# Two reorderings at the head of a mixture-of-experts stage: the first gate/up products on TensorE, the weight preparations on VectorE

## The reference

```
x = x + tanh(g_xattn[0]) * mamba(ctx, layernorm(x), ...)
# mixture of experts: E=64 experts, K=8 of them per token, at most CAP=64 tokens per expert
w, sel = top_k(softmax(layernorm(x) @ gate_w.T), 8); w = w / sum(w)
h   = silu(inp @ wg) * (inp @ wu)          # per expert: (64,256) @ (256,96), twice
out = h @ wd                               # (64,96) @ (96,256)
x = x + tanh(g_ffn[0]) * (sum over the chosen experts of w * out)
x = x + tanh(g_xattn[1]) * attention(layernorm(x), ctx, Wq, Wk, Wv, Wo)
# feed-forward with weight_quant: scale = 1 / mean(|w|); clip(round(w * scale), -1, 1) / scale
x = x + tanh(g_ffn[1]) * bitlinear(layernorm(gelu(silu(bitlinear(layernorm(x), w1)))), w2)
```

## Time and profile before

| | us |
|---|---|
| runs of the kernel | 674.95, 677.10, 678.04 (median 677.1) |
| the profiled execution | 675.54, of which the span is 673.8 |
| expert stage in the profile, from the first indices (218.9) to the last `combine` (329.6) | 110.7 |
| busy over the whole span: TensorE / VectorE / ScalarE / GpSimd | 503.6 / 507.5 / 355.7 / 275.9 |

### The profile page before, as it was taken

One profiled execution on the slowest core, in us unless ns is written; L12 is line 12 of the kernel. 1 busy time (PEld: TensorE's weight loads), 2 busy tenths in 40 slices (PEclk: granted clock), 3 DMA queues, 4 the chain that ended last, 5 costly groups with the idle time before them and its releaser, 6 DMA issues.

```text
span 673.8 us, 10758 instructions
## 1 busy us (share of the span) xinstructions
PE 503.6 (75%) x3144; PEld 371.6 (55%) x3144; DVE 507.5 (75%) x1328; ACT 355.7 (53%) x784; POOL 275.9 (41%) x261
## 2 busy tenths in 40 slices
PE   5935777778695488979779999999999997243232
PEld 3311222223285356757569999999999996022021
DVE  4277999999869856945447977977887886878854
ACT  2474555445176221221446766676676666485483
POOL 4016777788010743530068358538632331110100
PEclk9955999989898597999879999999999999665566
DMA  6907300000023399992412013103200000000000
GB/s 171 216 10 285 97 0 0 0 32 1 8 54 112 97 286 266 285 285 72 145 52 73 9 24 72 33 1 69 56 0 1 1 2 0 0 17 0 16 16 16
DMA packets 43794, 48.53 MB, mean 72 GB/s; under 512 B 5628, under 2 KB 40038, under 8 KB 43494
## 3 DMA queue, kind: packets, MB, share of 16 engines
q1 hardware_dynamic: 39910, 36.46, 19.0%
q0 software_dynamic: 3840, 11.54, 7.2%
HBM read 41.43 MB, written 6.56 MB: 71 GB/s over the span
## 4 chain that ended last, share of the span: by engine, by line
issue 33%; PE 20%; DVE 19%; POOL 14%; DMA 6%; ACT 5%; DVEq 1%; SPq 1%; POOLq 0%; ACTq 0%
DVE hst L1426 6%; POOL G L551 5%; POOL pn L567 5%; DMA wdn<-in_L_ffn_wd 4%; PE ps L1165 3%; PE ps L915 2%; PE ps L1130 2%; DVE hc L1435 2%; PE ps L1150 1%; POOL G L531 1%; PE ps L1206 1%; DVE ebuf L1559 1%; DVE ebuf L1558 1%; PE ps L1208 1%; PE ps L1207 1%
## 5 line engine op out<-in xcount | busy, mean ns | idle before, releaser
L567 POOL TENSOR_TENSOR pn<-pr,pinv 128x512 f32<-128x512 f32 x64 | 66.9, 1046 | 88.5 <-DVE pinv L1794 87.9
L966 PE MATMUL ps<-hc,ident 128*128 128x512 f32 x128 | 75.4, 679 | 29.0 <-DVE hc L1435 27.5
L472 POOL TENSOR_TENSOR dbu<-du,brow 128x512 f32<-128x512 f32 x64 | 80.6, 1270 | 24.7 <-DVE hst L1426 18.5
L1426 DVE TENSOR_TENSOR_SCAN hst<-ps,dbu 128x512 f32<-128x512 f32 x64 | 77.8, 1217 | 4.3 <-ACT ps L660 4.3
L660 ACT ACTIVATE ps<-dtv,amat 128x510 f32<-128x510 f32 x64 | 44.1, 689 | 51.7 <-DVE hst L1426 51.5
L531 POOL DMA_INDIRECT G<-token_rows,idx_x x32 | 42.3, 1323 | 69.2 <-issue 37.1
L802 ACT ACTIVATE pr<-ebuf,smin 128x256 f32<-128x256 f32 x128 | 63.5, 500 | 2.7 <-DVE smin L1785 2.7
L966 PEld LDWEIGHTS ps<-hc,ident 128*128 128x128 f32 x128 | 20.8, 201 | 70.4 <-DVE hc L1435 67.7
L1750 DVE TENSOR_TENSOR pT<-ps,pT 128x512 fp32r<-128x512 f32 x64 | 44.0, 687 | 15.8 <-ACT pT L810 14.9
L551 POOL DMA_INDIRECT G<-expert_out,idx_b x48 | 50.0, 1042 | 11.5 <-issue 11.5
L816 ACT ACTIVATE oT<-ps 128x256 fp32r<-128x256 f32 x64 | 24.6, 385 | 48.7 <-PE ps L1208 48.7
(11 more groups left out here) (295 smaller groups left out, 1551.1 us busy)
## 6 DMA issues: line engine op xcount, KB each, us to landing
wgu<-in_L_ffn_wg SPq DMA_DIRECT2D x15, 384.0 KB
wgu<-in_L_ffn_wu SPq DMA_DIRECT2D x15, 384.0 KB
wdn<-in_L_ffn_wd SPq DMA_DIRECT2D x15, 384.0 KB
expert_out<-xn SPq DMA_DIRECT2D x16, 256.0 KB
wq<-in_L_xattn_Wq SPq DMA_DIRECT2D x1, 2048.0 KB, 9.1
wo<-in_L_xattn_Wo SPq DMA_DIRECT2D x1, 2048.0 KB, 14.7
wo<-in_L_ffn_w SPq DMA_DIRECT2D x2, 1024.0 KB, 7.4
x<-in_x SPq DMA_DIRECT2D x1, 1024.0 KB, 6.6
```

The costliest lines, as they stand in the source:

```text
L472: nc.gpsimd.tensor_tensor(dbu[:, j, :], du[:, j % 2, 512 * hb:512 * hb + 512], brow[:, j // 2, :], ALU.mult).then_inc(pool_dbu, 1)
L567: nc.gpsimd.tensor_tensor(pn[:, h % 2], pr[:, h % 2], pinv[:, h % 2, :].unsqueeze(2).to_broadcast([P, 2, L]), ALU.mult)\
L966: pe.matmul(bank(2 + j % 2), ident[:], hc[:, j % 2, :], start=(isinstance(m, int) and m + k == 0), stop=(isinstance(m, int) and m + k == N ...
L1426: V.tensor_tensor_scan(hst[:, j, :], bank(j % 2), dbu[:, j, :], 0.0, ALU.mult, ALU.add)\
```

## The change

On TensorE, `gate_up(0)` stands directly behind `turn_rows(0)`, ahead of `turn_rows(1)`, and the product with `wabs` stands behind `turn_rows(1)`. On VectorE `folded_low(0)`, `folded_low(1)`, `weight_scales` and `ternary(0, .)` no longer stand ahead of the first `slot_shares`. `weight_scales` is now in step 0, `folded_low(0)` and `(1)` in the steps 3 and 4, the six passes of `ternary` in the steps 8, 9 and 10 (two in each), and `folded_low(2)` and `(3)` in the steps 11 and 12 (before: 9 and 10). `slot_tok` is counted by `idx_x_ready`, for which TensorE and `placed` now wait.

```diff
@@ -1181,15 +1181,17 @@
-            pe.wait_ge(wabs_ready, 1)
-            pe.matmul(ps[:, 7, 0:2], ones[:], wabs[:], start=True, stop=True).then_inc(summed, 1)
-            pe.wait_ge(idx_x_ready, 1)
+            pe.wait_ge(idx_x_ready, 2)
             turn_rows(0)
+            gate_up(0)
             for g in range(NG + 3):
                 if g + 1 < NG:
                     turn_rows(g + 1)
-                if g < NG:
+                if 0 < g < NG:
                     gate_up(g)
+                if g == 0:
+                    pe.wait_ge(wabs_ready, 1)
+                    pe.matmul(ps[:, 7, 0:2], ones[:], wabs[:], start=True, stop=True).then_inc(summed, 1)
                 if 1 <= g < NG + 1:
                     turn_h(g - 1)
@@ -1560,7 +1562,7 @@
-            chain.step(V.tensor_scalar(slot_tok, ps[:, 0, 0:E // 2], -1.0, float(B * L), ALU.mult, ALU.add))
+            V.tensor_scalar(slot_tok, ps[:, 0, 0:E // 2], -1.0, float(B * L), ALU.mult, ALU.add).then_inc(idx_x_ready, 1)
@@ -1645,6 +1647,7 @@
             def placed(g):
 
                 wait_count(dve, summed, g)
+                dve.wait_ge(idx_x_ready, 2)
@@ -1660,11 +1663,6 @@
             weight_sums()
-            folded_low(0)
-            folded_low(1)
-            weight_scales()
-            for k in range(3):
-                ternary(0, k)
             dve.wait_ge(d_rows, 64)
@@ -1675,6 +1673,7 @@
                 if g == 0:
+                    weight_scales()
                     choice_ids()
@@ -1682,10 +1681,13 @@
                 if g == NT:
                     choice_indices()
-                if 2 < g < 6:
-                    ternary(1, g - 3)
-                if 8 < g < 11:
-                    folded_low(g - 7)
+                if 7 < g < 11:
+                    for n in (2 * g - 16, 2 * g - 15):
+                        ternary(n // 3, n % 3)
+                if 2 < g < 5:
+                    folded_low(g - 3)
+                if 10 < g < 13:
+                    folded_low(g - 9)
                 placed(g)
                 take_out(g)
```

## The result

| | before | changed |
|---|---|---|
| median of the runs beside each other, us | 678.04 (15 runs) | 674.68 (15 runs) |
| ratio to before | | 0.9953, 95% interval 0.9933 to 0.9972 |
| the profiled execution, us (span) | 675.54 (673.8) | 674.02 (672.3) |
| stage in the profile, L1158 to the first L1722 (L1724), us | 218.45 to 329.59: 111.1 | 219.44 to 326.31: 106.9 |

The change takes 0.47% (0.28 to 0.67), or 3.2 us of 678. I had forecast 2.4 us and 674.7, and given "within 0.5%" most of the chance. The exact hit of 674.7 is partly luck: the median of before had moved from 677.1 to 678.0 meanwhile.

What follows compares the result with a forecast made beforehand. The stream of transfers, by when it begins to be full and whether it stays so, was taken to bound the stage. Terms -2.8 + 0.4 = -2.4 us gave 677.1 - 2.4 = 674.7 us, range 672.2 to 678.2.

Steps and rivals of the forecast that it cites:

- The bound: Whole stage: its end is set by when the stream of transfers begins to be full and whether it stays full.
- `gate_up(0)` first: TensorE, step 0: `gate_up(0)` ahead of `turn_rows(1)` ends 3.0 us earlier, and so does the load of step 4.
- The unstretched row fetches: GpSimd, stage head: indirect DMAs take 1.00 us without VectorE's passes; step 2's rows land at 229.9, not 233.25.
- Rival B: Stage head: nothing arrives, the rows of step 2 or 3 stay late; 677 us, chance 0.14.
- the first in a queue: GpSimd, stage head: other reading, the DMAs were slow for their queue place, not VectorE's passes; gain near 0.
- The clock and `gate_up(1)`: TensorE, stage head: load of step 5 leaves 2.1 to 3.4 us earlier, depending on the clock; 2.8 taken.
- Step 4's VectorE order: VectorE, step 4: `put(4)` comes 1.0 us later and holds step 11's load; price 0 to 1.0, 0.4 taken.
- ScalarE: Stage head: `gate(0)` starts at 232.5 as before behind the table load; hides nothing that is waited for.
- The signs: Changed profile: gate loads at 229.5 and 233.7 to 235.1, last weight wait ending about 298.4, `combine` 2 to 3 us earlier.
- A: Rival, stage: the early clock's 3.4 us had whole plus some 0.7 from a fuller stream; 673.0 us, chance 0.22.
- C: Rival, steps 3, 4 and 8: VectorE's delays hold SyncE's queue, 4.8 less 2.8, +2.0; 679.1 us, chance 0.09.

Runs made afterwards that it cites:

- e1: The kernel before with only TensorE's new order and the new count of `idx_x_ready`; ratio to before 1.0009.
- e4: The changed kernel with `folded_low(0)` and `(1)` back at the head, `ternary` still moved; ratio to before 0.9990.
- e12: The kernel before, unaltered, run again; ratio to before 0.9991.
- e2: The changed kernel with TensorE's old order, so VectorE's part alone; ratio to before 0.9965.
- e3: The changed kernel with `folded_low(0)` and `(1)` both in step 2, not in steps 3 and 4; ratio to before 0.9967.
- e11: The changed kernel with the edits of e5, e6 and e9 together; ratio to before 0.9955.
- e5: The changed kernel with 20 products whose results nobody uses ahead of `turn_rows(0)` on TensorE; ratio to before 0.9940.
- e6: The changed kernel with silu's table loaded early on ScalarE and `gate(0)` ahead of the copy of step 1's rows; ratio to before 0.9931.
- e8: The changed kernel, unaltered, run again in the second group of runs; ratio to before 0.9942.
- e13: The same kernel as e2, VectorE's part alone, run again; ratio to before 0.9950.
- e14: The changed kernel, unaltered, run a third time; ratio to before 0.9942.
- e9: The changed kernel with `folded_low(0)` ahead of `gated(0)`, the other three in steps 11 to 13, none in 3 and 4; ratio to before 0.9949.
- the first group: The four runs e1 to e4, on one chip; ratios to before 1.0009, 0.9965, 0.9967 and 0.9990.

## Why the prediction was right

**The bound.** Right. The last weight wait ended 4.3 us earlier on the stage's axis and the stage ended 4.3 us earlier. Over the runs, the ratio goes with the start of the stream. Where the load of step 7 leaves 26.2 to 27.5 us in (before, e1, e4, e12) it is 0.999 to 1.001; at 24.4 to 24.6 (e2, e3, e11) it is 0.9955 to 0.9967; at 22.4 to 23.4 (the change, e5, e6, e8, e13, e14) it is 0.993 to 0.995. From before to the change that is 3.3 us of head start for 3.2 to 4 us of time. e9 is the exception (26.0 and 0.9949), with its low-clock phase on that very load. The load times are from one profile each, so this is a trend, not a proof.

**`gate_up(0)` first.** The load of step 4 came 3.0 us earlier, as worked out. But e1 shows it worth nothing alone, and e13 beside e14 leaves it about 0.1% in company, not settled. My text gave the two parts one sum and did not say which of them carried it.

**The unstretched row fetches.** Right, and the heart of it: 1.00 us each, and with two passes put back (e4) the gain goes. e4 agrees with the rule that I had taken from the Trainium skill ("SBUF — State Buffer", section "SBUF: two separate sides"), that a VectorE operation with two SBUF inputs shuts out a GpSimd operation that reads SBUF: 2.33 and 1.90 beside such passes, 0.99 behind them. Rival B and the reading "the first in a queue" are out by the same rows. What the prediction did not have is the other half: e1 and e4 have the early load of step 4 too, and there the rows of step 2 landed 3.4 us after GpSimd's work and not 2.0. So far as these runs show, an early load pays if the rows of the next steps are fetched ahead of it.

**The clock and `gate_up(1)`.** This term was too small. I took 2.8, the middle of 2.1 and 3.4; in the pair of profiles the load of step 5 came 3.6 us earlier, which is outside these bounds. The clock gave 1.0 of it (2.83 against 1.82). The other 2.6 is the earlier start of `gate_up(1)` (13.3 us in, before 15.9), for which I had 2.1: the pieces ahead of it took 2.2 us and not 2.8, the product with `wabs` 0.3 of them and not 0.6. Over two profiles of before and three of the change the load of step 5 is at 17.0 to 18.7 against 14.4 to 15.1, and the load of step 7 is 3.0 to 3.7 us earlier.

**Step 4's VectorE order.** I took 0.4 us. The chain did run through it, with the DMA engines not full from 262 to 266, yet e9 takes the passes away and gains nothing. The price is 0 within the noise. The two mis-sized terms (2.8 for about 3.3, and 0.4 for 0) would account for the difference between 2.4 forecast and 3.2 measured; but the measured interval (1.9 to 4.5) holds both.

**ScalarE.** I had written that the late `gate(0)` hides nothing that is waited for. That was wrong: the profile has a wait for it, 1.2 us for the rows of step 4. e6 takes it away, for a gain too small to be seen.

**The signs.** On the axis of before, the two loads left at 229.6 and 233.6 (I had said 229.5, and 233.7 to 235.1), and no new wait for VectorE came in the steps 8 to 15. The last weight wait ended at 296.5 and not at 298.4, and the last `combine` came 4.3 us earlier and not 2 to 3. The share of the DMA engines did not stay at 1: it was 0.86 from 235 to 239 and 0.74 for 4 us behind `put(3)`, where I had allowed 1 us behind `put(4)`. The ends of my range, 672.2 and 678.2, do not follow from the times of A and C (673.0 and 679.1), so that the range held is a weak test.

**Rivals.** A (the early clock whole and a fuller stream) was right on the clock's part, and its 4.1 us is inside the measured interval. Its second half, better phases in mid-stage, is chance from run to run (0, 3.4 and 3.4 us in three profiles of the changed kernel). C (VectorE's later steps hold SyncE's queue): the gap of the DMA engines is there, its price is not.

**Still open.** The part behind the stage took 346.0, 346.2 and 346.8 us in the three profiles of the change, 344.2 and 345.9 in the two of before, and 343.8 in the four runs of the first group. No instruction of it differs. VectorE's part does not lengthen it, since e2 and e3 have that part and 343.8; nor does the low clock, which in that stretch lasted 94 us in the first profile of before and 87 us in that of the change. Why the stage's 4.2 to 6.5 us in the profiles are 3.2 to 4 in the ratios may lie there; no run was made for it.

## What to carry to other kernels

Where a ring of buffers feeds a stage that the DMA engines limit, the time is made at the start: find the first releases of the ring, and what they wait for, and look beyond the engine that issues them. Large VectorE passes in "idle" time are not free if GpSimd is making descriptors beside them: keep them out of a stretch in which somebody waits for its indirect DMAs. Fetch what TensorE needs next ahead of the large loads: in e1 the early load and late rows came together, and nothing was won. A piece on the chain in mid-stage is no cost if the next weight wait takes up the time; test it by moving the piece, not by reading the chain.

## What the runs showed of the hardware

- An indirect DMA of 128 rows took 0.99 to 1.3 us of GpSimd's time at the head of the stage, and 1.90 to 2.61 beside a VectorE pass of two SBUF inputs over 128x2048 elements (2.28 us). Beside the single-input passes of `ternary` in the changed kernel it took 2.12 and 1.68; beside the sums of `wabs` (2.28 us, one input) 1.00 to 1.3.
- In the steps 3 and 4 of the changed kernel the stretched DMAs (259.91 + 2.61 and 266.44 + 2.61) both ended 0.87 us after the end of the VectorE pass beside them (261.65 and 268.18), as if most of their work began when the pass was over; the VectorE passes themselves were no longer than alone.
- Rows fetched by an indirect DMA landed 1.9 to 2.1 us after its end when no weight load was on its way at that time (before, changed, e12, e13; once 2.9, in e2), and 3.4 to 3.9 us after it when a weight load of 768 KB had been started 0.6 to 2.1 us before that end (before, changed, e1, e4, e5, e12). That the load causes the delay is the likely reading; no run moved the load alone.
- In the two profiles of before, a full clock that came 5 us earlier (e12) changed only how long TensorE waited: the loads of the steps 6 and 7 left at 21.9 and 26.2 us in both.
